# First mixer: quarter-array products for the small doublings of the inverse, and state products ahead of query products

## The reference

```
S = S * exp(g_t)                       # S is 64 x 128
delta = (v_t - k_t @ S) * beta_t
S = S + outer(k_t, delta);   o_t = q_t @ S
```

## Time and profile before

| what | value |
|---|---|
| median of 3 runs | 5456.53 us |
| the profiled execution: span from first to last instruction | 5452.6 us |
| instructions | 104905 |
| PE (matmul) busy | 4831.1 us, 89% |
| PEld (weight load) busy | 3535.1 us, 65% |
| DVE busy | 3836.5 us, 70% |
| ACT busy | 2736.9 us, 50% |
| POOL busy | 2285.8 us, 42% |
| mean granted TensorE clock | 0.926 |

### The profile page before, as it was taken

The page is one execution under the profiler, slowest core; times in us unless marked ns, Lnnn a source line. Parts: engine busy times, 40 slices in busy tenths (PEclk is TensorE's granted clock), DMA queues, the critical chain, the costliest instruction groups (busy, mean ns, idle before and its releaser), DMA issues. The chain is left out here.

```text
span 5452.6 us, 104905 instructions
## 1 busy us (share of the span) xinstructions
PE 4831.1 (89%) x36890; PEld 3535.1 (65%) x36890; DVE 3836.5 (70%) x9111; ACT 2736.9 (50%) x6711; POOL 2285.8 (42%) x1860
## 2 busy tenths in 40 slices
PE   5999999999999999999889989984488778998998
PEld 3787777877777787777766556641156665654665
DVE  4766667777677766767578668746699657866874
ACT  2444445444544544545478658724400116875882
POOL 2434334344334434434267347514322116743751
PEclk7999999999999999999999999986699758998998
DMA  2000000000000000000100000000000000000000
GB/s 86 5 9 7 7 9 7 7 9 7 7 9 10 5 9 8 6 9 9 34 1 0 25 5 0 0 7 0 8 1 1 1 1 30 0 24 5 0 0 16
DMA packets 170085, 52.60 MB, mean 10 GB/s; under 512 B 142304, under 2 KB 166112, under 8 KB 168928
## 3 DMA queue, kind: packets, MB, share of 16 engines
q1 hardware_dynamic: 168160, 44.30, 3.7%
q10 hardware_dynamic: 1536, 3.21, 0.2%
HBM read 36.99 MB, written 10.49 MB: 9 GB/s over the span
## 5 line engine op out<-in xcount | busy, mean ns | idle before, releaser
L799 DVE SCALAR_TENSOR_TENSOR gd_qkT<-gd_ps,gd_w_qk,gd_qkT 128x256 f32<-128x256 f32 x768 | 367.2, 482 | 193.3 <-ACT gd_qkT L632 172.7
L984 POOL TENSOR_TENSOR gd_gV<-gd_g,cst 128x512 f32<-128x512 f32 x128 | 130.3, 1040 | 860.1 <-PE gd_ps L510 860.1
L417 PE MATMUL gd_ps<-gd_taps,gd_xwins 128*128 128x512 f32 x1024 | 465.3, 597 | 0.0
L676 ACT ACTIVATE gd_X<-gd_ps 128x512 f32<-128x512 f32 x384 | 201.1, 620 | 452.9 <-PE gd_ps L496 452.6
L1540 ACT ACTIVATE L_ffn_s<-L_ffn_s,L_ffn_nb,L_ffn_r 128x128 f32<-128x128 f32 x1024 | 419.4, 482 | 3.1
L1360 POOL TENSOR_TENSOR L_ffn_t<-L_ffn_t 128x512 f32<-128x512 f32 x128 | 190.2, 1486 | 391.8 <-DVE L_ffn_t L1581 391.8
L417 PEld LDWEIGHTS gd_ps<-gd_taps,gd_xwins 128*128 128x128 f32 x1024 | 192.8, 191 | 191.1 <-issue 185.6
L868 DVE TENSOR_TENSOR gd_Z<-gd_ps,cst 128x256 f32<-128x256 f32 x384 | 162.7, 424 | 129.6 <-PE gd_ps L512 111.1
L1579 DVE TENSOR_TENSOR L_ffn_t<-L_ffn_ps,L_ffn_sb_rope 128x512 f32<-128x512 f32 x256 | 176.8, 691 | 101.8 <-PE L_ffn_ps L1385 101.8
L521 PE MATMUL gd_ps<-gd_Z,gd_X 128*128 128x64 f32 x2048 | 239.2, 275 | 0.0
L512 PE MATMUL gd_ps<-gd_gV,gd_nA 128*128 128x64 f32 x2048 | 237.9, 275 | 0.0
(11 more groups left out here) (389 smaller groups left out, 13625.6 us busy)
## 6 DMA issues: line engine op xcount, KB each, us to landing
L_ffn_sb_rope<-in_rope SPq DMA_DIRECT2D x4, 2048.0 KB, 8.3
gd_tap_row<-in_L_attn_conv_v SPq DMA_DIRECT2D x2, 2048.0 KB, 15.6
gd_blocks<-gd_nA SPq DMA_DIRECT2D x256, 16.0 KB, 1.7
gd_Z<-gd_blocks SPq DMA_DIRECT2D x32, 128.0 KB, 2.0
gd_inverses<-gd_Z SPq DMA_DIRECT2D x32, 128.0 KB, 1.7
gd_gV<-gd_inverses SPq DMA_DIRECT2D x256, 16.0 KB, 1.9
L_ffn_sb_wqkv<-in_L_ffn_wqkv SPq DMA_DIRECT2D x4, 768.0 KB, 8.9
out<-out_tok SPq DMA_DIRECT2D x8, 256.0 KB, 2.6
```

The lines of the kernel that those rows point to most:

```text
L417: ins = pe.matmul(ps[4 + i % 2][:], xwin(j)[:, t:t + P], taps[:, t, 512 * i:512 * (i + 1)], start=(t == 0), stop=(t == TAPS - 1))
L676: act.activation(heads(X, gi).rearrange("p h x -> p (h x)"), ps[4 + gi][:], ACT.Copy).then_inc(x_s.sem, 1)
L799: ins = dve.scalar_tensor_tensor(produced(j, i), ps[6 + i % 2][:, P + t:P + t + WIDE], w_tap[:, at, t:t + 1], produced(j, i), ALU.mult, AL ...
```

## The change

The first two levels work on a compact form, Tc, a [128, 16, 64] tile that holds for each head only its two diagonal quarters, one above the other. A transpose now turns two heads at once (`half_turn`). Both products of a level are split into their quarters, each with 64 rows and 64 columns of the array and 32 columns streamed (`half_z`, `half_tz`); the first product of each such group of 16 takes 128 columns. The four groups of heads become two of 8, and DVE masks and adds for 8 heads at a time. The merge of the second level writes into the full Tm, in two instructions for each group. A new POOL instruction fills the other columns of Tm from Tc. The last level works on quarters too, and its two products are interleaved on PE. DVE's chain for the decays is cut into more parts. POOL sets Tc to zero beside Tm, and the DMA of the inverses goes to Tc. On PE the products of the keys with the state now stand ahead of those of the queries.

```diff
-LEVELS = [16, 32, 64]
+LEVELS = [16, 32]
...
-        cols = np.array([c for c in i if (c // s) % 2 == 0])
-        t[:, C_MERGE + 64 * n:C_MERGE + 64 * (n + 1)] = i[:, None] // s == cols[None, :] // s + 1
+        cols = np.array([c for c in range(HALF) if (c // s) % 2 == 0])
+        t[:, C_MERGE + 32 * n:C_MERGE + 32 * (n + 1)] = i[:, None] % HALF // s == cols[None, :] // s + 1
...
-        ps = [ctx.enter_context(nc.psum_tensor(f"gd_ps{i}", [P, 512], F32)) for i in range(8)]
+        banks = ctx.enter_context(nc.psum_tensor("gd_ps", [P, 8, 512], F32))
+        ps = [banks[:, i] for i in range(8)]
...
-        Tm, R = gV, v
+        Tm, Tc, R = gV, sb("Tc", [P, H, HALF]), v
         PT, yT, y, squares = decay, X, delta, X
+        Xc = X[:, 0:H // 2]
+        Zc = Z[:].rearrange("p h x -> p (h x)")[:, 0:2 * 8 * 32].rearrange("p (r k x) -> p r k x", r=2, k=H // 2)
...
-                    sp.wait_ge(*Tm_zero.now(n))
+                    sp.wait_ge(*Tc_zero.now(n))
...
-                        sp.dma_start(diagonal(Tm, q), inverse_dram[q].rearrange("h i j -> i h j")).then_inc(T_in.sem, 16)
+                        sp.dma_start(Tc[BASE * q:BASE * (q + 1), :, BASE * (q % 4):BASE * (q % 4 + 1)], inverse_dram[q].rearrange("h i j -> i h j")).then_inc(T_in.sem, 16)
...
                 def state_products(n, j):
+                    w(S_s.before(n))
...
-                            w(gate_out.now(n, 3)); w(S_s.before(n))
+                            w(gate_out.now(n, 3))
...
+                def half_turn(n, l, i):
+                    w(T16_s.now(n, i) if l else o1_s.now(n, i))
+                    for k in range(4):
+                        h = 8 * i + 2 * k
+                        ins = pe.transpose(ps[4 + i][:, P * k:P * (k + 1)], Tc[:, h:h + 2].rearrange("p h x -> p (h x)"), ident)
+                    ins.then_inc(xc_mm.sem, 1)
+
+                def half_z(n, l, i):
+                    if l == 0:
+                        w(R_s.now(n, 2 * i + 1))
+                    for k in range(4):
+                        for r in range(2):
+                            for c in range(2):
+                                h = 8 * i + 2 * k + c
+                                part = slice(0, P) if k == r == c == 0 else None
+                                ins = pe.matmul(banks[part or rows(c), 2 * i + r, 32 * k:32 * (k + 1)], nA[rows(r), h, part or rows(r)],
+                                                even(Tc, h, h + 1, LEVELS[l])[rows(r), 0], start=True, stop=True)
+                    ins.then_inc(zc_mm.sem, 1)
+
+                def half_tz(n, l, i):
+                    w(xc_s.now(n, 2 * l + i)); w(zc_s.now(n, 2 * l + i))
+                    for k in range(4):
+                        for c in range(2):
+                            for r in range(2):
+                                part = slice(0, P) if k == r == c == 0 else rows(r)
+                                ins = pe.matmul(banks[part, 2 * i + c, 32 * k:32 * (k + 1)], Xc[rows(c), 4 * i + k, part],
+                                                Zc[rows(c), r, 4 * i + k], start=True, stop=True)
+                    ins.then_inc(tzc_mm.sem, 1)
+
                 def turn_T(n, gi):
+                    w(odd_s.now(n)); w(T32_s.now(n, 2 * (gi // 2) + 1))
                     for k in range(HG):
-                        ins = pe.transpose(ps[4 + gi][:, P * k:P * (k + 1)], Tm[:, HG * gi + k], ident)
+                        ins = pe.transpose(ps[(6, 7, 4, 5)[gi]][:, P * k:P * (k + 1)], Tm[:, HG * gi + k], ident)
                     ins.then_inc(x_mm.sem, 1)
+
+                def last_z(n, gi, k):
+                    h = HG * gi + k
+                    part = slice(HALF if k else 0, P)
+                    return pe.matmul(ps[gi][part, 64 * k:64 * (k + 1)], nA[0:HALF, h, part], Tm[0:HALF, h, 0:HALF], start=True, stop=True)
+
+                def last_tz(n, gi, k):
+                    h = HG * gi + k
+                    n = 1 if k else 2
+                    return pe.matmul(ps[gi][0:HALF * n, 64 * k:64 * (k + 1)], Z[HALF:P, h:h + n].rearrange("p h x -> p (h x)"), X[HALF:P, h, HALF:P], start=True, stop=True)
 
                 def solve(n):
                     w(T_in.now(n))
+                    for l in range(len(LEVELS)):
+                        for i in range(2):
+                            half_turn(n, l, i)
+                            half_z(n, l, i)
+                        for i in range(2):
+                            half_tz(n, l, i)
+                    for gi in range(2):
+                        turn_T(n, gi)
+                    for gi in range(2):
+                        for k in range(HG):
+                            ins = last_z(n, gi, k)
+                        ins.then_inc(z_mm.sem, 1)
+                    for gi in range(2, G):
+                        turn_T(n, gi)
+                    for gi in range(2, G):
+                        w(z_s.now(n, gi - 2)); w(x_s.now(n, gi - 2))
+                        for k in range(HG):
+                            first = last_z(n, gi, k)
+                            second = last_tz(n, gi - 2, k)
+                        first.then_inc(z_mm.sem, 1)
+                        second.then_inc(tz_mm.sem, 1)
+                    for gi in range(2, G):
+                        w(z_s.now(n, gi)); w(x_s.now(n, gi))
+                        for k in range(HG):
+                            ins = last_tz(n, gi, k)
+                        ins.then_inc(tz_mm.sem, 1)
                     for gi in range(G):
...
+                        w(T64_s.now(n, gi))
...
+                    state_products(n, j)
                     query_products(n, j)
-                    state_products(n, j)
                     solve(n)
...
+                def half_turned(n, l, i):
+                    w(xc_mm.now(n, 2 * l + i))
+                    act.activation(Xc[:, 4 * i:4 * (i + 1)].rearrange("p h x -> p (h x)"), ps[4 + i], ACT.Copy).then_inc(xc_s.sem, 1)
+
                 def late(n):
+                    for i in range(2):
+                        from_state(n, 2 * i)
+                        from_state(n, 2 * i + 1)
+                        half_turned(n, 0, i)
+                    for i in range(2):
+                        half_turned(n, 1, i)
                     for gi in range(G):
+                        w(x_mm.now(n, gi))
+                        act.activation(heads(X, gi).rearrange("p h x -> p (h x)"), ps[(6, 7, 4, 5)[gi]], ACT.Copy).then_inc(x_s.sem, 1)
...
+                def mask_z(n, l, i):
+                    w(zc_mm.now(n, 2 * l + i))
+                    mask = cst[:, C_MERGE + 32 * l:C_MERGE + 32 * (l + 1)].unsqueeze(1).unsqueeze(1).to_broadcast([P, 2, 4, 32])
+                    dve.tensor_tensor(Zc[:, :, 4 * i:4 * (i + 1)], products(i).rearrange("p r (k x) -> p r k x", x=32), mask, ALU.mult).then_inc(zc_s.sem, 1)
+
+                def merge16(n, i):
+                    w(tzc_mm.now(n, i))
+                    old = even(Tc, 8 * i, 8 * (i + 1), 16).rearrange("p (k c) n s -> p k c n s", c=2)
+                    new = products(i).rearrange("p c (k n s) -> p k c n s", n=2, s=16)
+                    dve.tensor_tensor(old, new, old, ALU.add).then_inc(T16_s.sem, 1)
+
+                def merge32(n, i):
+                    w(tzc_mm.now(n, 2 + i)); w(Tm_zero.now(n))
+                    for r in range(2):
+                        old = by_pair(Tc[rows(r), 8 * i:8 * (i + 1), 0:32], 2)
+                        new = products(i, rows(r)).rearrange("p c (k x) -> p k c x", x=32)
+                        dve.tensor_tensor(by_pair(Tm[rows(r), 8 * i:8 * (i + 1), HALF * r:HALF * r + 32], 2), new, old, ALU.add).then_inc(T32_s.sem, 1)
+
+                def last_z(n, gi):
+                    w(z_mm.now(n, gi))
+                    dve.tensor_copy(heads(Z, gi)[HALF:P].rearrange("p h x -> p (h x)"), ps[gi][HALF:P, 0:256]).then_inc(z_s.sem, 1)
+
+                def merge64(n, gi):
+                    w(tz_mm.now(n, gi))
+                    dve.tensor_copy(heads(X, gi)[0:HALF, :, HALF:P],
+                                    ps[gi][0:HALF, 0:256].rearrange("p (h x) -> p h x", h=HG)).then_inc(T64_s.sem, 1)
 
...
-                    level(n, 0)
+                    for gi in range(G):
+                        residues(n, gi)
+                    mask_z(n, 0, 0)
+                    mask_z(n, 0, 1)
+                    merge16(n, 0)
+                    merge16(n, 1)
                     if follows:
-                        decays_first(n + 1)
-                    level(n, 1)
+                        decays_ratio(n + 1)
+                    mask_z(n, 1, 0)
+                    mask_z(n, 1, 1)
                     if follows:
-                        decays_second(n + 1, j + 1, s)
-                    level(n, 2)
+                        decays_series((13, 11))
+                    merge32(n, 0)
+                    merge32(n, 1)
+                    if follows:
+                        decays_series((9, 7, 5, 3))
```

(64 more changed lines are left out.)

38 lines of the change are left out of this document (17 added, 21 removed).

## The result

The changed kernel takes 5426.65 us (median of 10 runs, 5409.51 to 5445.98) against 5455.88 for the kernel before (10 runs): a ratio of 0.9935 [0.9914, 0.9955], 29 us faster. The forecast was 123 us faster, 5333; the median lies 94 us above it and 1.65 us above the range.

The account below looks back on a forecast made before the run. PE's queue was taken to bound the kernel (busy 89% of the span, 95% of a chunk). 3.75 us from the solve plus 0.1 from the swap, 3.85 a chunk over 32 chunks, gave 123 us: 5333, range 5289 to 5425.

Parts of the forecast that it names:

- the sum: Whole first mixer: 3.75 us from the solve plus 0.1 from the swap, 3.85 a chunk, 32 chunks, 123 us saved.
- the first rival: Small levels: a group of four quarter products can't go under 0.11 us; only 45 us saved, 5411; chance 25%.
- Price of a quarter product: Small levels on PE: a group of four takes 0.06 us, held by weight loads; a block of 16 takes 1.1.
- Changes of shape: Solve on PE: 0.2 us each; small levels 11.2 us in all, saving 6.6; last level 8.1 against 5.5.
- The slower rival: Solve on PE: changes of shape dearer than seen, at 0.40 us each 82 us slower, 5538; chance 10%.
- Waits inside the solve: PE waits 0.35 us in level two for DVE's chain beside POOL, about 0.1 in the last level; solve 19.75.
- The second rival: Small levels: hand-overs between PE, DVE and ACT have half the cover, 1.6 us a chunk given back; 5385; chance 15%.
- State products first: Before the solve: state products fill PE's 0.69 us wait for the gate; worth 0.1 us a chunk, bounds 0 and 0.65.
- the ACT wait: Before the first turn: PE waits 0.5 us for ACT's copies of the query products, which now stand right before it.
- R "is ready": Level one: Z waits for R two groups earlier, but R starts 1.9 us earlier by the swap, so no wait.

Follow-up runs that it names:

- e1_wide64: The changed kernel with each small-level product streaming its 32 columns twice (64 columns, only the first 32 read): 5295.63 us, 0.9697 of the kernel before.
- e4_before_32: The kernel before, with its doublings of 16 and 32 streaming, masking and merging only the first 32 of 64 columns: 5792.9 us, ratio 1.0617.

## Why the prediction was wrong

- **The step that failed is the sum.** It took 3.85 us a chunk times 32, all valued at the clock of the earlier trace rows, 1.00. Nothing in the working asked what the change does to that clock. The new products stream 32 columns each; with them the clock fell in 25 of 32 solves and stayed low behind them, which cost some 187 us in the profile (150 + 37). e1_wide64 and e4_before_32 show that the columns do it: more of them in the changed kernel bring 131 us, fewer in the kernel before cost 332, with nothing else moved on PE. None of the rivals had it. That the time came out near the first rival's 5411 and the top of the range is chance: its floor is in no record, as the next point shows.
- *Price of a quarter product:* right, and a little too dear. A block of Z takes 0.92 (1121.98 to 1122.90, the next turn), 1.1 forecast. Twenty records inside it, the last of them 0.22 long, show groups of four (0.49 - 0.22) / 19 x 4 = 0.06 us apart:

```profile
1122.31 0.49 PE L523 MATMUL gd_ps<-gd_Tc,gd_nA 64*64 64x32 f32 x20
```

The first rival is refuted. The rule behind it, the floor of about 25 ns from start to start in the Trainium skill ("TensorE: Matmul & The Clock Gate", section "Wait — 56ns, not 53.3ns?"), does not hold for these records, which follow each other in 14 ns; the measurement decides.
- *Changes of shape:* right in the main, and too dear. Level one took 4.90 (5.6), level two 5.68 with its waits (5.6 + 0.35), the last level 7.15 (8.1 + 0.1), which is the term furthest off. The slower rival is refuted.
- *Waits inside the solve:* the mechanism was right. PE waits 0.48 (forecast 0.35) at the first TZ of level two, because a link that reads two SBUF tensors stands beside POOL's odd block. Timeline of DVE, then of POOL:

```profile
1127.27 1.60 DVE L838 TENSOR_TENSOR gd_tmp<-gd_e_ab,gd_tmp 128x16 f32<-128x16 f32 x1
```

```profile
1126.95 1.89 POOL L1118 TENSOR_TENSOR gd_gV<-gd_Tc,cst 128x1024 f32<-128x1024 f32 x1 [14.07 <-DVE gd_Tc L938]
```

POOL took 1.89 (2.1 forecast from L984 in the earlier trace rows). The second rival, the chain in PE's place, is not borne out: no other wait between the engines in this solve's two small levels, up to the last level's first turn, exceeds 0.21.
- *State products first:* the ACT wait came as laid out (0.42; 0.5 forecast), but the sentence that R "is ready" hid the swap's worth. In the changed kernel the swap keeps PE off a wait for R, with which the clock falls in all 32 solves instead of 25: 184 us, not 3. That the wait itself takes the clock down is argued, not shown. In the kernel before, the swap alone costs 18.5 us instead of saving 3, since the wait for the gate comes back at the first turns.

At 1.00 the parts sum to 17.7, so each was a little too dear and the forecast's solve 2 us too long; the clock took back far more than that.

## What to carry to other kernels

Before products are made smaller, ask what the engine's clock does: a busy PE with products of few columns can lose half of its clock, and the work behind it pays too. Look at the granted clock of the stage, in many chunks, not at the busy share; and if extra columns cost little, as here (1.05 us for a block instead of 1.00), try streaming the same ones twice. A small VectorE instruction that reads two SBUF tensors can cost nearly as much as the GpSimd instruction that it meets, so moving it can move the wait to a dearer place.

## What the runs showed of the hardware

- With products of 32 columns the granted clock fell both as 64x64 quarters (in 25 of 32 solves) and as full 128x128 ones (32 of 32), to 0.50 in the stretches shown; the same products with 64 columns kept 1.00 in 28 and in 27 solves, quarters with 128 columns in 26.
- 64x64 records on alternating quarters start 14 ns apart on the mean (20 of them); on the full array 32 columns are no faster than 64 (0.109 and 0.110).
- A small VectorE instruction with two SBUF inputs grew from 0.17 to 1.60 and to 1.02 us beside GpSimd instructions of 1.89 and 1.04. The Trainium skill ("GPSIMD Engine Reference", section "1. Specifications") names this contention for two SBUF inputs; these rows agree.
